# AdaLN-conditioned ternary FFN on one core: loops of four engines written out, x halves, gathers and an opening reordered

## The chip, the cores and the metric

The kernel runs on one core of one Trainium2 chip. The metric is device microseconds of an execution: 975.07 us is the median of 3 runs of the kernel before (974.96 to 975.81). Engines are named as in the profile: PE (matmul), PEld (its weight loads), DVE, ACT, POOL, SP, the last three also as issuers of DMAs.

## The reference, cut to what matters

```
w  = weights[conditions]                       # B=128 conditions pick from 200 matrices 64x64
c  = einsum('bct,bcd->bdt', x, w)              # x: 128 x 64 x 512
h  = gelu(einsum(c, ternary(W1)) + b1)         # W1: 2048 x 512
y  = einsum(h, ternary(W2)) + b2               # W2: 512 x 2048
scale = max|y| / 7 + 1e-8                      # one scale for the whole tensor
out = x + clip(round(y / scale), -7, 7) * scale
```

`ternary(W)` is alpha * sign(W) where |W| exceeds 0.05 * max|W|, and 0 elsewhere; alpha is the mean of |W| over the elements that pass. The scale needs every y before any output can be written, so the kernel has a long middle that makes y, and a tail that rounds, adds x and stores.

## The kernel before, in words

The 8192 rows (128 samples x 64) are cut in 16 blocks of 512 rows. For each block PE does a **conditioning** (line 500, in two halves of four samples, 32 matmuls of 128x64 each: psC from xs and ws), a **first product** (line 520, 128 matmuls of 128x512, 16 hidden tiles, four PSUM banks in turn) and a **second product** (lines 530, 581 and 674, 128 matmuls of 128x512). For blocks 2 to 12 the second product is made by seven half-size products in Strassen's manner (line 632, `seven`), 7 times 32 matmuls of 128x256, from sums of quarters of h that DVE and ACT build beside the first product (`hidden_seven`). Values are split in a high and a low fp16 part (`high_x`, `low_x`, `high_c`, `low_c`, and so on: ACT makes the high part, DVE the low part).

Steps are numbered by i; step i uses block i and conditions block i + 1. `seven_step(i, s)` on PE is: condition(i+1, 0), three products, one more, condition(i+1, 1), the other products. Then the first product of block i + 1 follows. PE's program is written out in full; in SP, POOL, ACT and DVE the steps i = 2 to 10 are one `Fori` loop with the step number in a register.

What each step needs from elsewhere:

- **x halves.** SP loads x of a half block (`load_half`, two DMAs of 512 KB, line 309) into `yx` (first halves) or `xd1`, which is block 14 of y (second halves of the loop). In the opening all of half blocks 0 to 4 (counted from block 2) go into `yx` one after another, each load waiting for `x_split` of the half before, which is the end of `low_x` on DVE. ACT's `sum_x` waits for the load, POOL's `all_max_x` for that, DVE's `scale_xw`, ACT's `high_x` and DVE's `low_x` follow.
- **Gathers.** POOL gathers the 64x64 matrices of four samples at a time (`gather`, lines 401 and 405: one copy of indices, four indirect DMAs) into `wg`, half 0 or half 1. In `seven_step` the order is: all_max_x(2i), gather of half 1 for block i + 2, all_max_x(2i+1), wait for x_split 2i+1, gather of half 0 for block i + 3. For the two last such steps (`LATE_X`, i = 11 and 12) POOL waits for x_split 2i and gathers half 1 first.
- **t sums.** `hidden_seven` on ACT may begin only when DVE has passed the end of the step before (line 1354 raises t_added, raw_split and m_read after `block_step(1)`).

The **opening**: ACT's queue loads the condition numbers broadcast to 128 partitions (`condb`, line 706) and b1, SP loads W1 in eight pieces, x of blocks 0 and 1 (`load_direct`), W2 and x half 0. DVE turns the condition numbers into row indices (lines 1047 to 1054), POOL gathers for blocks 0 and 1 (`gather_direct`, line 411). DVE takes max|W1| (line 1060), makes masks (line 1079) and ternary weights (line 1087); ACT takes |W1| (774), sums of relu (778), spreads the gathered matrices (721, 722) and makes the high part of c0 (716), DVE the low part (997). POOL's `all_max(xwb_part ...)` gives the bound for c0's scale. PE does condition_direct of block 0, counts the masks (`count1`, line 541), tile 0 of the first product, condition_direct of block 1, and so on.

The **tail**: the output is made in `PIECES` in block order. A piece is rounded (ACT line 915, or DVE line 1407 for pieces 0, 1 and 3), x is added (DVE line 1420), and SP stores it (line 392). `CUT` says which blocks are cut: block 0 in four pieces, blocks 1, 11 and 12 in two, the others are one piece of 1 MB. ACT's queue loads x of the last three blocks (line 913) into the places of blocks 0 to 2, each ahead of the last piece of the block two further on and after that earlier block's own addition.

Of the kernel before, what the change touches and what calls it, by code (L numbers as in the profile page):

```python
# [8 lines left out]
I32 = mybir.dt.int32  # L9
# [9 lines left out]
def build(nc, x, cond, wcond, W1, b1, W2, b2, out):  # L19
# [47 lines left out]
    with ctx:  # L67
# [6 lines left out]
        def sem(name):  # L74
            return ctx.enter_context(nc.semaphore(name))
# [22 lines left out]
        odd_i = odd[:, 2 * BB * C:].bitcast(I32)  # L98
        condb, idx, ids = odd_i[:, 0:B], odd_i[:, B:2 * B], odd_i[:, 2 * B:2 * B + BB]
        idsd = odd_i[:, 2 * B + BB:2 * B + BB + DIRECT * RT].rearrange("p (b r) -> p b r", b=DIRECT)  # L100
# [22 lines left out]
        CUT = {0: [(slice(m, m + 1), slice(n, n + 1)) for m in (0, 1) for n in (0, 1)],  # L123
               1: [(slice(m, m + 1), ALL) for m in (0, 1)],
               11: [(slice(m, m + 1), ALL) for m in (0, 1)],
               12: [(slice(m, m + 1), ALL) for m in (0, 1)]}
# [74 lines left out]

        idt = g[:, 3, 0:B].bitcast(I32)
        slots = iter(range(128))
# [29 lines left out]
        psY = ps[:, HB + 2:, :]  # L233
        psC0 = psY[:, :, :].rearrange("p i (k r) -> p (i k) r", k=KT // 2)
        psN1, psN2 = psH[:, HB - 1, :], ps[:, HB, 0:1]
        psY0 = [psY[:, 0, :], psY[:, 1, :], psH[:, 2, :], psH[:, 3, :]]
# [12 lines left out]
        w_gathered = [sem("w_gathered0"), sem("w_gathered1")]  # L249
        pool_waited = sem("pool_waited")  # L250
        consts_made, idx_made, ids_made = sem("consts_made"), sem("idx_made"), sem("ids_made")
        zero_made = sem("zero_made")
# [48 lines left out]
        def _(sp):  # L301
# [96 lines left out]
        def _(pool):  # L398
# [17 lines left out]
            gather_direct(0, range(RT))  # L416
            gather_direct(1, range(0, 2))

# [26 lines left out]
            all_max_x(1)  # L445

            def columns(b):
                return idx[:, bass.ds(b * BB, BB)]

            def block_step(i):  # L450
# [20 lines left out]
            gather(4, columns(4), [0])  # L471
            with pool.Fori(2, NS) as i:
                seven_step(i)
# [15 lines left out]
        def _(pe):  # L489
# [56 lines left out]
            def count2(c):  # L546
# [16 lines left out]
            for j in range(HT):  # L563
                if j == 0:
                    pe.wait_ge(t1_begun, 1)
                else:
                    pe.wait_ge(t1_made, j // HC + 1)
                if j == HB - 1:
                    pe.wait_ge(n_read, 1)
                first(0, j, wait_bank=j >= HB, wait_c=False)  # L570
                if j == 0:
                    pe.wait_ge(xdirect_loaded[1], 16)
                    pe.wait_ge(w_spread, 2)
                    condition_direct(1, 0, psC)
                    condition_direct(1, 1, psC0)
# [129 lines left out]
        def _(act):  # L705
            act.dma_start(condb[:, :], cond.rearrange("(a b) -> a b", a=1).to_broadcast([P, B])).then_inc(cond_loaded, 16)
            act.dma_start(b1t[:, :], b1).then_inc(b1_loaded, 16)
# [79 lines left out]
            for c in range(LOADS):  # L787
                absolute(c)
            act.dma_start(b2b[:, :], b2.rearrange("(a n) -> a n", a=1).to_broadcast([P, T])).then_inc(b2_loaded, 16)
            act.wait_ge(diagonal_cleared, 1)  # L790
# [13 lines left out]
            relu1(2)  # L804
            relu1(3)
            act.wait_ge(relu_summed, WCH)

# [57 lines left out]
            def seven_step(i, s):  # L865
                high_c(i + 1, 0)
                high_t(s, HALF_H - 1)
                sum_x(0, loads=s + 5)
                high_x(2 * i, 0)
                high_c(i + 1, 1)  # L870
                sum_x(1, xd1, xd1_loaded, s + 1)
# [23 lines left out]
            for i in range(2 + NS, NB - 2):  # L895
                second_step(i, 2 * i - (NS + 1), xd=xlate[0])
                hidden(i + 1, rb=i + 1 - NS)
# [21 lines left out]
        def _(dve):  # L919
# [126 lines left out]
            dve.wait_ge(cond_loaded, 16)  # L1046
            link(nc.vector.tensor_scalar(idt, condb[:, :], 0.0, float(S), ALU.is_lt, ALU.mult))
            link(nc.vector.tensor_tensor(idt, idt, condb[:, :], ALU.add))
# [13 lines left out]
            for c in range(LOADS):  # L1062
                last = max_w1(c)
                if c == 0:
                    dve.wait_ge(b1_loaded, 16)
                    nc.vector.tensor_reduce(xwb[:, 2:3], b1t[:, :], AX.X, ALU.max, apply_absolute_value=True)
# [46 lines left out]
            ternary1(2)  # L1113
            dve.wait_ge(relu_summed, WCH)
# [9 lines left out]
            link(nc.vector.tensor_scalar(alpha1d, alpha1, 2.0, None, ALU.mult))  # L1124
            scale_h(link, direct=True)

            def max_w2(c):
# [66 lines left out]
            def beside_second(j):  # L1194
# [4 lines left out]
                if j == 9:  # L1199
                    low_x(1, 1)  # L1200
                    scale_c(link)
# [146 lines left out]

            block_step(1, 1, *tiles_of(1), link, beside=last_sums)

# [4 lines left out]
            dve.sem_inc(m_read, 1)  # L1355

            def in_loop(i, begin, count):
                done = [0]

                def lk(ins):  # L1360
                    done[0] += 1
                    ins.then_inc(dve_step, 1)
                    dve.wait_ge(dve_step, count * i + (steps[0] - count * begin + done[0]))

                return lk, done

# [9 lines left out]
            hidden_seven(2, 0, link)  # L1376
            STEPS = 18
            with dve.Fori(2, NS) as i:
                lk, done = in_loop(i, 2, STEPS)
                seven_step(i, i - 2, *quarter_of(i), lk)  # L1380
                hidden_seven(i + 1, i - 1, lk)
                assert done[0] == STEPS, done
            steps[0] += STEPS * (NS - 2)
            owed = seven_step_late(LATE_X[0], NS - 2, *quarter_of(LATE_X[0], yx[:, :, :]), link)
# [76 lines left out]
```

## Time and profile before

| what | value |
|---|---|
| median of 3 runs | 975.07 us (974.96 to 975.81) |
| profiled execution | 974.98 us |
| its span, first to last instruction | 973.2 us |
| mean granted TensorE clock | 0.972 |
| PE busy | 892.0 us (92%) |
| DVE busy | 759.4 us (78%) |
| ACT busy | 638.2 us (66%) |
| POOL busy | 163.1 us (17%) |
| DMA bytes | 78.57 MB |

The profile is of one execution. Its busy shares are means over stages with different limits, so the stages are read one by one: in the timeline and the chain of waits each row has its start in us from the span's start, its length, its engine and line, and in brackets the idle time of the engine just before and what ended it. A matmul's end is modelled; the distance between the starts of two groups is the safer measure.

### The profile page before, as it was taken

How to read it: one execution, taken by the hardware profiler on the slowest of the kernel's cores; microseconds unless marked ns; L12 is line 12 of the kernel's file. 1: busy time of each engine (PE TensorE's matmuls, PEld its weight loads, DVE VectorE, ACT ScalarE, POOL GpSimd, SP SyncE). 2: the span in 40 equal slices, each digit the busy share in tenths (PEclk: the TensorE clock that was granted, in tenths of full speed). 3: DMA queues.
4: the chain of work that ended last, by engine and by line, in shares of the span. 5: the costliest groups of instructions: out<-in, count | busy, mean ns of one | idle time of the engine just before them, and what ended most of it. 6: DMA issues, size and time to landing. Idle time of an engine off the chain costs nothing.

```text
span 973.2 us, 16130 instructions
## 1 busy us (share of the span) xinstructions
PE 892.0 (92%) x6192; PEld 542.2 (56%) x6192; DVE 759.4 (78%) x1245; ACT 638.2 (66%) x718; POOL 163.1 (17%) x185
## 2 busy tenths in 40 slices
PE   2999999999999999999999999999999999999600
PEld 2544444766758484766758484857667444444300
DVE  7997859899797979799897979898797465433494
ACT  6787946668494958668494958666685836335191
POOL 4400231120303012121304021140410300000000
PEclk9999999999999999999999999999999999999855
DMA  9501222220304031221304040203013230204899
GB/s 338 171 3 32 50 62 47 51 49 18 81 1 97 1 74 25 50 50 27 72 1 98 1 87 12 50 11 74 22 30 64 54 87 1 87 1 156 310 388 398
DMA packets 24508, 78.57 MB, mean 81 GB/s; under 512 B 3968, under 2 KB 4096, under 8 KB 23936
## 3 DMA queue, kind: packets, MB, share of 16 engines
q1 hardware_dynamic: 19360, 70.26, 24.6%
q0 software_dynamic: 3840, 3.94, 1.6%
q10 hardware_dynamic: 1248, 3.48, 1.0%
q8 instruction: 48, 0.79, 0.3%
q14 instruction: 12, 0.10, 0.0%
HBM read 60.89 MB, written 16.78 MB: 80 GB/s over the span
## 4 chain that ended last, share of the span: by engine, by line
PE 61%; issue 18%; DVE 11%; ACT 4%; DMA 3%; POOL 1%; DVEq 0%; SPq 0%; ACTq 0%; POOLq 0%
PE ps L520 31%; PE ps L632 27%; PE ps L500 2%; ACT y L784 1%; DMA yx<-in_x 1%; DVE hs L981 1%; DVE st L1060 1%; DVE st L1129 1%; ACT xs L735 1%; DVE y L1250 1%; DMA y<-in_x 1%; DVE xs L1026 1%; DVE y L1420 1%; ACT g L752 1%; DMA odd<-in_itok_B 1%
## 5 line engine op out<-in xcount | busy, mean ns | idle before, releaser
L520 PE MATMUL ps<-yc,wts 128*128 128x512 f16 x2048 | 445.0, 379 | 1.9 <-ACT g L856 1.4
L520 PEld LDWEIGHTS ps<-yc,wts 128*128 128x128 fp8e4 x2048 | 200.2, 98 | 241.6 <-ACT g L856 1.9
L856 ACT ACTIVATE g<-ps,b1t,st 128x512 f32<-128x512 f32 x176 | 134.3, 770 | 43.6 <-PE ps L520 33.7
L405 POOL DMA_INDIRECT odd<-in_L_cond_weights,odd x112 | 133.9, 1195 | 50.4 <-issue 33.2
L632 PE MATMUL ps<-y,hs 128*128 128x256 fp8e4 x1056 | 118.9, 273 | 0.0
L1235 DVE SCALAR_TENSOR_TENSOR hs<-y,st,hs 128x1024 f16<-128x1024 f32 x88 | 112.5, 1278 | 0.0
L632 PEld LDWEIGHTS ps<-y,hs 128*128 128x128 f16 x1056 | 102.6, 98 | 11.7
L846 ACT ACTIVATE hs<-y,st 128x1024 f16<-128x1024 f32 x88 | 100.0, 1137 | 10.7 <-DVE y L1259 10.7
L422 POOL PARTITION_ALL_REDUCE st<-st x32 | 13.8, 430 | 532.5 <-DVE st L1003 404.1
L752 ACT ACTIVATE g<-ps,b1t,st 128x512 f32<-128x512 f32 x80 | 62.2, 778 | 58.4 <-PE ps L520 48.2
L981 DVE SCALAR_TENSOR_TENSOR hs<-g,st,hs 128x512 f16<-128x512 f32 x80 | 58.7, 750 | 47.7 <-ACT hs L757 46.6
L1250 DVE SCALAR_TENSOR_TENSOR y<-g,st,y 128x768 f16<-128x768 f32 x88 | 89.0, 1011 | 0.2 <-ACT y L861 0.2
L861 ACT ACTIVATE y<-g,st 128x768 f16<-128x768 f32 x88 | 82.4, 936 | 4.1 <-DVE odd L1028 1.3
L530 PE MATMUL ps<-wts,hs 128*128 128x512 fp8e4 x384 | 83.9, 379 | 0.0
L632 PE MATMUL ps<-wts,y 128*128 128x256 fp8e4 x704 | 78.8, 273 | 0.4 <-DVE y L1250 0.3
L632 PEld LDWEIGHTS ps<-wts,y 128*128 128x128 f16 x704 | 68.1, 98 | 8.4 <-DVE y L1250 0.4
L728 ACT ACTIVATE xs<-y,st 128x2048 f16<-128x2048 f32 x15 | 30.0, 2001 | 57.6 <-DVE st L1011 57.6
L1245 DVE TENSOR_TENSOR y<-g 128x512 f32<-128x512 f32 x88 | 60.3, 685 | 2.4 <-ACT g L856 1.1
L746 ACT ACTIVATE yc<-ps,st 128x1024 f16<-128x1024 f32 x28 | 30.9, 1103 | 47.4 <-PE ps L500 47.4
L530 PEld LDWEIGHTS ps<-wts,hs 128*128 128x128 f16 x384 | 37.1, 98 | 43.9
L757 ACT ACTIVATE hs<-g,st 128x512 f16<-128x512 f32 x80 | 56.7, 715 | 0.0
L1270 DVE SCALAR_TENSOR_TENSOR y<-ps,st,b2b 128x512 f32 (+1 forms) x40 | 29.9, 748 | 25.8 <-PE ps L632 25.7
(167 smaller groups left out, 981.1 us busy)
## 6 DMA issues: line engine op xcount, KB each, us to landing
y<-in_x SPq DMA_DIRECT2D x30, 512.0 KB, 7.1
yx<-in_x SPq DMA_DIRECT2D x26, 512.0 KB
y<-in_L_ffn_W SPq DMA_DIRECT2D x8, 512.0 KB, 7.5
y<-in_L_ffn_W SPq DMA_DIRECT2D x4, 1024.0 KB, 20.5
hs<-in_x SPq DMA_DIRECT2D x8, 512.0 KB, 5.0
out<-hs SPq DMA_DIRECT2D x8, 512.0 KB, 12.4
y<-in_x ACTq DMA_DIRECT2D x3, 1024.0 KB, 10.2
out<-y SPq DMA_DIRECT2D x3, 1024.0 KB, 13.9
```

What stands on the lines that cost most here:

```text
L405: nc.gpsimd.indirect_dma_start(out=wg[:, j, :], out_offset=None, in_=w_rows[:, :], in_offset=bass.IndirectOffsetOnAxis(ap=ids[:, j:j + 1], ...
L520: last = nc.tensor.matmul(psH[:, j % HB, :], weights, csp[:, a, k, :], start=(k == 0 and a == 0), stop=(k == KT - 1 and a == 1))
L530: last = nc.tensor.matmul(psY[:, r % 2, :], hsp[:, a, j, r * P:(r + 1) * P], T2T[:, j, :], start=(j == 0 and a == 0), stop=(j == HT - 1 an ...
L632: last = nc.tensor.matmul(psM[bank][:, t * HALF_T:(t + 1) * HALF_T], rows[:, a, p, at:at + P], weights[:, p, :], start=(first_of_bank and ...
L752: nc.scalar.activation(g[:, j % HB, :], psH[:, j % HB, :], ACT.Gelu, bias=b1t[:, j:j + 1], scale=ascale).then_inc(g_made, 1)
L846: nc.scalar.activation(told[:, 0, p, :], tsum[:, p % 2, :], ACT.Copy, scale=s_h).then_inc(thi_made, 1)
L856: nc.scalar.activation(g[:, q % HB, :], psH[:, q % HB, :], ACT.Gelu, bias=b1t[:, q:q + 1], scale=ascale).then_inc(g_made, 1)
L861: nc.scalar.activation(raw[:, :, 0, p, :], gp[:, p % 2, HALF_T:].rearrange("p (q w) -> p q w", q=3), ACT.Copy, scale=s_h).then_inc(rhi_mad ...
L981: nc.vector.scalar_tensor_tensor(out=hsp[:, 1, j, :], in0=g[:, j % HB, :], scalar=s_h, in1=hsp[:, 0, j, :], op0=ALU.mult, op1=ALU.subtract ...
L1235: nc.vector.scalar_tensor_tensor(out=told[:, 1, p, :], in0=tsum[:, p % 2, :], scalar=s_h, in1=told[:, 0, p, :], op0=ALU.mult, op1=ALU.subt ...
L1245: nc.vector.tensor_tensor(at[:, 0:2 * HALF_T].rearrange("p (s t) -> p s t", s=2), gp[:, p % 2:p % 2 + 1, 0:HALF_T].to_broadcast([P, 2, HAL ...
L1250: nc.vector.scalar_tensor_tensor(out=raw[:, :, 1, p, :], in0=gp[:, p % 2, HALF_T:].rearrange("p (q w) -> p q w", q=3), scalar=s_h, in1=raw ...
```

## The change

- The `Fori` loops of SP, POOL, ACT and DVE over steps 2 to 10 become Python loops, so that their instructions are written out.
- x: half 1 goes to `xd1` as soon as ACT's four relu sums are made (they used that place); then half 2 to `yx` after x_split 1, half 3 to `xd1` after x_split 2, half 4 to `yx` after x_split 3.
- POOL: the gather of half 0 for block 3 comes after x_split 1, ahead of all_max_x(1); in `seven_step` the gather of half 1 for block i + 2 comes first, after a wait for x_split 2i.
- Step 1 of ACT and DVE is written out in an order of its own; DVE's `max_y(1, 0)`, `last_sums(0)` and `max_w(3)` change places.
- Opening: condition numbers are loaded once, into one partition; three DVE operations on that row; a matmul with one row of ones spreads it over 128 partitions in PSUM (`psIds`); DVE's last index operation reads it there. POOL gathers three tiles of block 1 before the maxima, and the fourth behind `all_max(xwb_part ...)`. ACT's load of b2 moves behind relu1(3). `mask_w1(3)` moves behind c0's low part, `count1(3)` behind tile 0 of the first product, `ternary1(2)` behind `scale_h`, the maximum of b1 behind the second W1 piece.
- Tail: blocks 2 and 3 are cut in two pieces each.

```diff
@@ CUT
                1: [(slice(m, m + 1), ALL) for m in (0, 1)],
+               2: [(slice(m, m + 1), ALL) for m in (0, 1)],
+               3: [(slice(m, m + 1), ALL) for m in (0, 1)],
@@ SP
             load_half(2 * DIRECT)
-            for n in range(1, 5):
+            sp.wait_ge(relu_summed, WCH)
+            load_half(1 + 2 * DIRECT, xd1, xd1_loaded)
+            for n in range(1, 4):
                 sp.wait_ge(x_split, n)
-                load_half(n + 2 * DIRECT)
-            with sp.Fori(2, NS - 1) as i:
+                if n % 2:
+                    load_half(n + 1 + 2 * DIRECT)
+                else:
+                    load_half(n + 1 + 2 * DIRECT, xd1, xd1_loaded)
+            for i in range(2, NS - 1):
@@ POOL
             gather_direct(0, range(RT))
-            gather_direct(1, range(0, 2))
+            gather_direct(1, range(0, 3))
...
             all_max(max1_part, 1, m1r, m1, max1_all)
-            gather_direct(1, range(2, RT))
             pool.wait_ge(x0_summed, 1)
             all_max(xwb_part, 1, xwbr, xwb, xwb_all)
+            gather_direct(1, range(3, RT))
...
             all_max_x(0)
+            pool.wait_ge(x_split, 1)
+            gather(2, columns(3), [0])
             all_max_x(1)
...
             def seven_step(i):
+                pool.wait_ge(x_split, 2 * i)
+                gather(2 * i + 1, columns(i + 2), [1])
                 all_max_x(2 * i)
-                gather(2 * i + 1, columns(i + 2), [1])
                 all_max_x(2 * i + 1)
                 pool.wait_ge(x_split, 2 * i + 1)
                 gather(2 * i + 2, columns(i + 3), [0])
-            pool.wait_ge(x_split, 2)
-            gather(2, columns(3), [0])
             all_max_x(2)
...
-            with pool.Fori(2, NS) as i:
+            for i in range(2, NS):
                 seven_step(i)
@@ PE
+            pe.wait_ge(id_row_made, 1)
+            nc.tensor.matmul(psIds, ones_f[0:1, :], id_row, start=True, stop=True).then_inc(ids_spread, 1)
...
-            for c in range(WCH):
+            for c in range(WCH - 1):
                 count1(c)
+            pe.wait_ge(idx_made, 1)
...
                 if j == 0:
+                    count1(WCH - 1)
                     pe.wait_ge(xdirect_loaded[1], 16)
@@ ACT
-            act.dma_start(condb[:, :], cond.rearrange("(a b) -> a b", a=1).to_broadcast([P, B])).then_inc(cond_loaded, 16)
+            act.dma_start(cond_row, cond.rearrange("(a b) -> a b", a=1)).then_inc(cond_loaded, 16)
...
                 if j == 4:
-                    sum_x(1, loads=2)
+                    sum_x(1, xd1, xd1_loaded, 1)
                 if j == 8:
-                    high_x(1, 1)
+                    high_x(1, 1, xd1)
...
-            second_step(1, 3)
+            high_c(2, 0)
+            sum_x(0, loads=2)
+            high_x(2, 0)
+            high_c(2, 1)
+            sum_x(1, xd1, xd1_loaded, 2)
+            high_x(3, 1, xd1)
             hidden_seven(2, 0)
-            with act.Fori(2, NS) as i:
+            for i in range(2, NS):
@@ DVE
-            link(nc.vector.tensor_scalar(idt, idt, 0.0, float(S - 1), ALU.max, ALU.min))
-            link(nc.vector.tensor_scalar(idx[:, :], idt, float(C), pc64, ALU.mult, ALU.add))
+            nc.vector.tensor_scalar(id_row, idt, 0.0, float(S - 1), ALU.max, ALU.min).then_inc(id_row_made, 1)
+            dve.wait_ge(ids_spread, 1)
+            link(nc.vector.tensor_scalar(idx[:, :], psIds, float(C), pc64, ALU.mult, ALU.add))
...
-            mask_w1(3)
             ternary1(0, slice(0, 1), t1_begun)
             dve.wait_ge(cscale_ready, 1)
             low_c0(0, psC)
             low_c0(1, psC0)
+            mask_w1(3)
...
-            block_step(1, 1, *tiles_of(1), link, beside=last_sums)
+            scale_h(link)
+            low_c(2, 0)
+            max_w(2, 0, 3)
+            scale_xw(2, 0, link)
+            store_y(1, 0, tile_y(0))
+            low_x(2, 0)
+            low_c(2, 1)
+            max_y(1, 0, tile_y(0), slot(0))
+            store_y(1, 1, tile_y(1))
+            max_y(1, 1, tile_y(1), slot(1))
+            last_sums(0)
+            max_w(3, 1, 3)
+            scale_xw(3, 1, link)
+            store_y(1, 2, tile_y(2))
+            max_y(1, 2, tile_y(2), slot(2))
+            low_x(3, 1, xd1)
+            scale_c(link)
+            last_sums(1)
+            store_y(1, 3, tile_y(3))
+            max_y(1, 3, tile_y(3), slot(3))
...
-            with dve.Fori(2, NS) as i:
-                lk, done = in_loop(i, 2, STEPS)
-                seven_step(i, i - 2, *quarter_of(i), lk)
-                hidden_seven(i + 1, i - 1, lk)
+            for i in range(2, NS):
+                seven_step(i, i - 2, *quarter_of(i), link)
+                hidden_seven(i + 1, i - 1, link)
```

## Rows read from the trace of the kernel before

**Rows 1.** The page, busy time of PE (and its weight loads).

```profile
PE 892.0 (92%) x6192; PEld 542.2 (56%) x6192; DVE 759.4 (78%) x1245; ACT 638.2 (66%) x718; POOL 163.1 (17%) x185
```

**Rows 2.** Waits of PE: line, releaser, us in total, times, longest.

```profile
PE ps L520 <- ACT g L856: 1.4, 1, 1.4
PE ps L581 <- ACT g L752: 0.8, 2, 0.6
```

**Rows 3.** The chain of waits: start us, us, what; from step 2 to step 12.

```profile
191.81 0.81 PE ps L500 x27
...
194.05 10.48 PE ps L632 x96
204.53 27.63 PE ps L520 x128
232.16 0.93 PE ps L500 x32
...
639.38 27.63 PE ps L520 x128
...
693.33 27.63 PE ps L520 x128
...
747.27 27.64 PE ps L520 x128
```

**Rows 4.** Timeline of PE, from step 1 to step 2.

```profile
146.85 7.07 PE L520 MATMUL ps<-yc,wts 128*128 128x512 f16 x32
...
204.37 27.79 PE L520 MATMUL ps<-yc,wts 128*128 128x512 f16 x128
```

**Rows 5.** The chain of waits inside step 1.

```profile
133.12 6.96 DMA yx<-in_x
140.10 2.01 ACT xs L735 x2
...
143.84 2.30 DVE y L1192
...
154.47 1.46 ACT g L856 x2
```

**Rows 6.** DMA queues while step 3 conditions, 246.4 to 248.7 us.

```profile
q0 software_dynamic: 104, 0.10, 17.5%
```

**Rows 7.** DMA queues while step 11 conditions, 681.2 to 682.9 us.

```profile
q1 hardware_dynamic: 86, 0.31, 88.5%
```

**Rows 8.** Timeline of POOL ahead of step 11: first and last gather of half 1.

```profile
644.01 0.97 POOL L405 DMA_INDIRECT odd<-in_L_cond_weights,odd  x1 [0.81 <-POOL odd L401]
...
648.27 1.09 POOL L405 DMA_INDIRECT odd<-in_L_cond_weights,odd  x1 [0.30 <-issue]
```

**Rows 9.** Stretches of the tail: engines busy, PEclk, DMA share, GB/s.

```profile
926.00:930.00 4.00, 0.00 (x0) 0.00 (x0) 3.85 (x2) 3.17 (x3) 0.00 (x0) 0.50 0.95 273
930.00:972.00 42.00, 0.00 (x0) 0.00 (x0) 28.34 (x15) 23.35 (x14) 0.00 (x0) 0.50 1.02 419
```

**Rows 10.** Timeline of DVE in the tail: block 2's addition.

```profile
926.12 2.35 DVE L1420 SCALAR_TENSOR_TENSOR xs<-y,st,xs 128x2048 f32<-128x2048 int16 x1 [0.26 <-ACT y L915]
```

**Rows 11.** Stretches of the opening, columns as in Rows 9.

```profile
2.50:5.50 3.00, 0.00 (x0) 0.00 (x0) 0.87 (x5) 0.65 (x2) 0.00 (x0) 1.00 0.67 188
5.50:8.50 3.00, 0.00 (x0) 0.00 (x0) 2.20 (x7) 2.09 (x2) 0.58 (x1) 1.00 1.03 401
```

**Rows 12.** Timeline of the opening.

```profile
18.70 5.34 PE L508 MATMUL ps<-odd,hs 128*128 128x128 f32 x32 [18.70 <-DMA hs<-in_x]
...
19.88 2.41 POOL L411 DMA_INDIRECT odd<-in_L_cond_weights,odd  x1 [0.30 <-issue]
...
27.73 0.41 ACT L721 ACTIVATE odd<-odd 64x256 f32<-64x256 f32 x1
```

**Rows 13.** Waits of DVE between 195 and 640 us.

```profile
DVE y L1270 <- PE ps L632: 41.8, 25, 2.9
```

**Rows 14.** The page, instruction packets of the queue that isn't PE's.

```profile
q14 instruction: 12, 0.10, 0.0%
```

More of the change, by code:

```diff
@@ L98, in build @@
         odd_i = odd[:, 2 * BB * C:].bitcast(I32)
-        condb, idx, ids = odd_i[:, 0:B], odd_i[:, B:2 * B], odd_i[:, 2 * B:2 * B + BB]
+        cond_row, idx, ids = odd_i[0:1, 0:B], odd_i[:, B:2 * B], odd_i[:, 2 * B:2 * B + BB]
         idsd = odd_i[:, 2 * B + BB:2 * B + BB + DIRECT * RT].rearrange("p (b r) -> p b r", b=DIRECT)
@@ L200, in build @@
         xtail += [place(y[:, b, :, :].rearrange("p r t -> p (r t)")) for b in range(NB - XS)]
-        idt = g[:, 3, 0:B].bitcast(I32)
+        idt, id_row = g[0:1, 3, 0:B].bitcast(I32), g[0:1, 3, B:2 * B]
         slots = iter(range(128))
@@ L234, in build @@
         psC0 = psY[:, :, :].rearrange("p i (k r) -> p (i k) r", k=KT // 2)
+        psIds = psH[:, 0, 0:B]
         psN1, psN2 = psH[:, HB - 1, :], ps[:, HB, 0:1]
@@ L250, in build @@
         pool_waited = sem("pool_waited")
+        id_row_made, ids_spread = sem("id_row_made"), sem("ids_spread")
         consts_made, idx_made, ids_made = sem("consts_made"), sem("idx_made"), sem("ids_made")
@@ L444, in _ @@
             all_max_x(0)
-            all_max_x(1)
             def columns(b):
                 return idx[:, bass.ds(b * BB, BB)]
+            pool.wait_ge(x_split, 1)
+            gather(2, columns(3), [0])
+            all_max_x(1)
             def block_step(i):
@@ L788, in _ @@
                 absolute(c)
-            act.dma_start(b2b[:, :], b2.rearrange("(a n) -> a n", a=1).to_broadcast([P, T])).then_inc(b2_loaded, 16)
             act.wait_ge(diagonal_cleared, 1)
@@ L805, in _ @@
             relu1(3)
+            act.dma_start(b2b[:, :], b2.rearrange("(a n) -> a n", a=1).to_broadcast([P, T])).then_inc(b2_loaded, 16)
             act.wait_ge(relu_summed, WCH)
@@ L867, in seven_step @@
                 high_t(s, HALF_H - 1)
-                sum_x(0, loads=s + 5)
+                sum_x(0, loads=s + 3)
                 high_x(2 * i, 0)
                 high_c(i + 1, 1)
-                sum_x(1, xd1, xd1_loaded, s + 1)
+                sum_x(1, xd1, xd1_loaded, s + 3)
                 high_x(2 * i + 1, 1, xd1)
-            second_step(1, 3)
+            high_c(2, 0)
[4 more added lines that the diff above has]
+            high_x(3, 1, xd1)
             hidden_seven(2, 0)
-            with act.Fori(2, NS) as i:
+            for i in range(2, NS):
                 seven_step(i, i - 2)
@@ L895, in _ @@
             for i in range(2 + NS, NB - 2):
-                second_step(i, 2 * i - (NS + 1), xd=xlate[0])
+                second_step(i, 2 * i - (NS + 3), xd=xlate[0])
                 hidden(i + 1, rb=i + 1 - NS)
@@ L1046, in _ @@
             dve.wait_ge(cond_loaded, 16)
-            link(nc.vector.tensor_scalar(idt, condb[:, :], 0.0, float(S), ALU.is_lt, ALU.mult))
-            link(nc.vector.tensor_tensor(idt, idt, condb[:, :], ALU.add))
-            link(nc.vector.tensor_scalar(idt, idt, 0.0, float(S - 1), ALU.max, ALU.min))
-            link(nc.vector.tensor_scalar(idx[:, :], idt, float(C), pc64, ALU.mult, ALU.add))
+            link(nc.vector.tensor_scalar(idt, cond_row, 0.0, float(S), ALU.is_lt, ALU.mult))
+            link(nc.vector.tensor_tensor(idt, idt, cond_row, ALU.add))
+            nc.vector.tensor_scalar(id_row, idt, 0.0, float(S - 1), ALU.max, ALU.min).then_inc(id_row_made, 1)
+            dve.wait_ge(ids_spread, 1)
+            link(nc.vector.tensor_scalar(idx[:, :], psIds, float(C), pc64, ALU.mult, ALU.add))
             by_tile = idx[:, 0:DIRECT * BB].rearrange("p (b r s) -> p s b r", b=DIRECT, s=2)
@@ L1063, in _ @@
                 last = max_w1(c)
-                if c == 0:
+                if c == 1:
                     dve.wait_ge(b1_loaded, 16)
@@ L1112, in _ @@
             ternary1(1)
-            ternary1(2)
             dve.wait_ge(relu_summed, WCH)
@@ L1125, in _ @@
             scale_h(link, direct=True)
+            ternary1(2)
             def max_w2(c):
@@ L1199, in beside_second @@
                 if j == 9:
-                    low_x(1, 1)
+                    low_x(1, 1, xd1)
                     scale_c(link)
@@ L1347, in last_sums @@
                     nc.vector.tensor_tensor(wsum[:, 3], A12, wsum[:, 1], ALU.subtract, saturate=False).then_inc(w2_summed, 1)
-            block_step(1, 1, *tiles_of(1), link, beside=last_sums)
+            tile_y, slot = tiles_of(1)
+            scale_h(link)
[18 more added lines that the diff above has]
+            max_y(1, 3, tile_y(3), slot(3))
             dve.wait_ge(h_split, 2 * HT)
@@ L1355, in _ @@
             dve.sem_inc(m_read, 1)
[L1357 to L1365, printed above, removed]
             def quarter_of(b, place=None):
@@ L1376, in _ @@
             hidden_seven(2, 0, link)
-            STEPS = 18
-            with dve.Fori(2, NS) as i:
-                lk, done = in_loop(i, 2, STEPS)
-                seven_step(i, i - 2, *quarter_of(i), lk)
-                hidden_seven(i + 1, i - 1, lk)
-                assert done[0] == STEPS, done
-            steps[0] += STEPS * (NS - 2)
+            for i in range(2, NS):
+                seven_step(i, i - 2, *quarter_of(i), link)
+                hidden_seven(i + 1, i - 1, link)
             owed = seven_step_late(LATE_X[0], NS - 2, *quarter_of(LATE_X[0], yx[:, :, :]), link)
```

## The prediction

> **What bounds the kernel now.** I read the busy times first, then PE's waits, then the chain of waits, and last the timelines around each place where PE stood. PE is busy 92% of the span [rows 1]. It starts at 18.70 us, when x of block 0 has landed [rows 12], and from then to its last product it hardly stands: its waits on other engines that matter are one of 1.4 us and two of 0.8 us together [rows 2]. So an edit counts only if it lets PE start sooner, fills a hole in PE's row, or shortens the tail behind PE; whatever other engines gain counts nothing by itself.
>
> The holes that PE's list of waits does not name are read from the distance between first products. From 639.38 to 693.33 and on to 747.27 a step takes 53.95 and 53.94 us: the clean step. From 204.53 to 639.38 there are eight steps, 434.85 us, where eight clean ones take 431.56: 3.29 us of holes [rows 3]. The step before is longer still: 146.85 to 204.37, 57.52 us, 3.57 too many [rows 4]. Inside it the second conditioning takes 194.05 - 191.81 = 2.24 us where an undisturbed one takes 0.93, so 1.31 of the 3.57 lie there; the other 2.26 lie ahead of it [rows 3].
>
> **The gathers.** In steps 2 to 10 POOL's gather of half 1 runs beside the second conditioning: 104 of its packets pass in 2.3 us around that of step 3 [rows 6]. In step 11, where POOL gathers half 1 well ahead (644.01 to 649.4) [rows 8], the x load keeps the DMA engines 88.5% busy beside the conditioning and no gather packet is there [rows 7], and that step is clean. So I put 3.29 + 1.31 = 4.60 us on the gathers, nine conditionings, about 0.5 each. The new order in `seven_step` is the one that steps 11 and 12 have: the gather of half 1 starts as soon as DVE has finished with that half, tens of us ahead of the conditioning, as in step 11 (649.4 against 681.2 or later). The instructions are the same. In front of POOL's next maximum there are now four more gathers, about 5 us, but that maximum waits for an ACT sum that comes much later. Term: 4.60 us; below, 0 if the cause is another.
>
> Trainium skill, SBUF — State Buffer, section "SBUF: two separate sides": engines and DMAs reach the memory by ports of their own, and a transfer cannot slow an engine. By that, gathered data landing would not hold PE, and this term would be 0. The rows of steps 3 and 11 speak for a tie to the gathers by whatever path, not necessarily the memory; I go with the rows and keep the rule as a rival.
>
> **Second x halves.** Step 1's chain is serial: a load of x half 3 that starts at 133.12 and lands at 140.08, ACT's sum of 2.01, scale, high and low part, two DVE sums of 2.30 each, then ACT's first gelu at 154.47 [rows 5]. PE has made four banks by then: 146.85 plus a quarter of 27.8 is 153.8, and it stands 1.4 us [rows 2, 4]; the rest of the 2.26 are small waits in the following products, because DVE and ACT are still behind. After the change half 3 is asked for at x_split 2, one half sooner, into a place of its own. What is late next: POOL's gather of half 1 for block 3, still issued behind this step's conditioning, now beside the load of half 4. If it lands as late as the x half does today (140.08), the sum of 2.01 and one DVE sum of 2.30 no longer stand behind it; with about 1 us back for the maximum of w, the gelu starts near 151.2. It needs to be done by 153.8. So all of 2.26 goes; the other bound, 0, needs the gather 3 us later than that.
>
> **Tail.** Behind PE the end is set by DMAs: 419 GB/s from 930 on, but 273 from 926 to 930, where only loads run while block 2's single piece is being added, 2.35 us [rows 9, 10]. Halved, its first 512 KB can leave half of 2.35, 1.2 us, earlier, and 1.2 x (419 - 273) / 419 = 0.4 us of transfer time comes back. At best the whole stretch runs at 419, 4 x 146 / 419 = 1.4. The loads of the last x blocks are asked for up to 0.5 us later, because ACT now does half pieces ahead of them: at worst -0.2. I take 0.4, the value of the one piece that moves.
>
> **Opening.** (a) The condition numbers, 128 rows of them, go beside W1's first pieces: from 2.5 to 5.5 us the DMAs move 188 GB/s, and 401 afterwards [rows 11]. At the full rate the loads would be 3 x 213 / 401 = 1.6 us ahead, and PE's start waits for such a load [rows 12]. But part of the slow stretch may be the start itself: 0 to 1.6, I take half, 0.8. The hop over PE and PSUM (an operation that no row shows, bounded by 0 and the 2.4 us that gathers have in hand) only delays gathers that nothing waits for: they start sooner than today. (b) The eighth gather moves behind `all_max(xwb)`: today it is issued at 19.88 and read at 27.73 without idle time before it [rows 12], so it takes at most 7.85 us to land. All_max, which runs behind it today at 22.3, goes first; the gather is then issued between 20.3 and 22.7. I take 21.2, since ACT's sum over x is then what all_max waits for; it lands by 29.1, up to 1.4 late for ACT's spread, and so for the relu sums, alpha and DVE's ternary weights, which PE's second product waits for. Between 0 and -1.4; I take -0.5, nearer to 0 since the landing came some time before the read. b2's later load is needed much later, and masks, counts and ternary parts are the same instructions in another order. Sum: +0.3, from -1.4 to +1.6.
>
> Trainium skill, DMA: Bandwidth & Descriptors, section "Queues, rings and completion order": each engine takes turns between queues packet by packet. By that the eighth gather would not stand behind the W2 load, (b) would cost nothing and the sum would be 0.5 us better; no row here shows the landing itself.
>
> **Written-out loops.** PE had no loop. The other four lose their branches, which costs or gains nothing as long as they keep ahead of PE; DVE alone stood 41.8 us waiting for PE's products between 195 and 640 [rows 13]. Term 0.
>
> **Sum.** 4.60 + 2.26 + 0.4 + 0.3 = 7.56. The profiled execution took 974.98 us, 1.8 more than its span, and gives 967.4; the median of the runs is 0.09 higher, so 967.5.
>
> **Rivals.**
> 1. The holes in the conditionings have another cause and stay: 967.5 + 4.6 = 972.1. For it: a coincidence in time is all that the rows show. Against: steps 11 and 12 are clean under the very order that is now used everywhere. The page on SBUF would have it so. Chance 0.09.
> 2. Step 1 stays late: the gather for half 1 of block 3 lands behind the load of half 4, PE stands again for its 2.3: 969.8. Against: 3 us in hand. Chance 0.08.
> 3. The opening loses: W1 starts no sooner and the eighth gather holds ACT by its full 1.4: 967.5 + 0.3 + 1.4 = 969.2. Chance 0.10.
> 4. Slower. Written out, the instruction streams of ACT and DVE in steps 2 to 10 must be fetched anew in every step, where the loops came back to code already there; today 12 such packets carry 0.10 MB in the whole run [rows 14]. If each step's fetch held DVE or ACT beyond what they have in hand, PE would stand in all nine steps. DVE's waits give 41.8 / 9 = 4.6 us in hand a step [rows 13]; a hold of 5.8 would cost 1.2 a step, 967.5 + 9 x 1.2 = 978.3. It turns the sign from 0.85 a step beyond that. Against: the written-out opening and tail show no DVE or ACT waits of such a size without a named releaser. Chance 0.04.
>
> **Chances.** The forecast has 0.69, with an own range of 966.1 to 969.0. What a measurement of this kernel can tell from no change is about 0.2%, 1.95 us, so faster means under 973.1. Rival 1 is faster mostly, with its neighbours in "same": faster 0.92, same 0.04, slower 0.04. For 8 in 10 I reach over rivals 2 and 3, to 970.2, and down to 966.0, which needs the opening at its better bound.
>
> **What would show it.** Right: every second conditioning of steps 2 to 10 at 0.93 us and all first products 53.9 us apart; no PE wait on ACT's gelu near 153; store rate in the first 10 us of the tail higher by a third in one 4 us stretch; PE's first matmul a little ahead of 18.70. Wrong: holes of 0.3 to 0.7 us left in the conditionings without gather packets beside them (rival 1); a gelu after 153.8 (rival 2); ACT idle before its second spread (rival 3); DVE or ACT rows with idle time that no other engine released, once a step (rival 4). The prediction fails if the time is above 970.2.

## The result, and the profile after

After: 967.99 us median of four runs (967.76 to 968.14), before 975.02 beside it (974.93 to 975.81): ratio 0.9926, 95% interval 0.9909 to 0.9943. The forecast was 967.5, with 966.0 to 970.2. The profiled execution took 968.06, its span 966.1; all comparisons of traces below are between spans.

The page first: PE has the same work but for two matmul records of the hop (L569, the matmul that spreads the condition numbers), and 1.0 us less of modelled busy time [rows 1]; the rest of the 7.1 us that the span lost was idle.

```profile
PE 891.0 (92%) x6194; PEld 542.5 (56%) x6194; DVE 762.2 (79%) x1247; ACT 639.9 (66%) x720; POOL 164.9 (17%) x185
```

PE's waits. The two holes named in [rows 2] were L520 waiting for ACT's gelu (1.4) and L581 (0.8); L533 and L599 are these lines now. The 1.4 is gone; what is left lies ahead of 62 us (L569 stands for the condition numbers and L521 for x, both at the start).

```profile
PE ps L521 <- DMA hs<-in_x: 12.2, 1, 12.2
PE ps L569 <- DVE g L1072: 4.2, 1, 4.2
PE ps L599 <- ACT g L770: 1.1, 2, 0.9
PE ps L599 <- issue: 0.6, 1, 0.6
PE ps L533 <- issue: 0.2, 1, 0.2
```

The chain of waits (start, us), first products L533 and second conditionings L513, against [rows 3].

```profile
146.46 27.63 PE ps L533 x128
...
188.99 0.93 PE ps L513 x32
200.40 27.63 PE ps L533 x128
...
242.94 0.93 PE ps L513 x32
254.35 27.63 PE ps L533 x128
...
685.92 27.63 PE ps L533 x128
...
739.87 27.64 PE ps L533 x128
```

Every step from 146 to 740 us is now 53.94 or 53.95 long, the length that steps 11 and 12 had before, and all conditionings take 0.93. Two marks on PE divide the 7.1 us. The first is the point from which block 0's second product runs on: that product begins at 58.45 (before 59.27), stands for ACT twice, and goes on steadily from its 13th matmul. The second is the start of the last product of all. Before, then after:

```profile
63.04 18.30 PE L581 MATMUL ps<-wts,hs 128*128 128x512 fp8e4 x84 [0.24 <-ACT g L752]
...
888.98 27.79 PE L674 MATMUL ps<-wts,hs 128*128 128x512 fp8e4 x128
```

```profile
62.49 18.30 PE L599 MATMUL ps<-wts,hs 128*128 128x512 fp8e4 x84 [0.24 <-ACT g L770]
...
881.57 27.79 PE L692 MATMUL ps<-wts,hs 128*128 128x512 fp8e4 x128
```

Opening 0.55, middle 6.86, tail -0.3. The last is no more than noise: from the start of the last product to the end it is 84.52 us here, 84.01 in the second trace of the same kernel (`e10_after_again`), and 84.18 before.

Step 1, against [rows 5]: ACT's gelu starts at 149.66 instead of 154.47. DVE waits 2.22 us there for POOL's gather, as the prediction said would be late next, and is still over 3 us ahead of PE's need.

```profile
149.66 1.45 ACT L874 ACTIVATE g<-ps,b1t,st 128x512 f32<-128x512 f32 x2 [6.86 <-DVEq L1398]
```

```profile
138.57 0.42 DVE L1026 TENSOR_REDUCE st<-odd 128x1 f32<-128x256 f32 x1 [2.22 <-DMA odd<-in_L_cond_weights,odd]
```

The opening: stretches (last column GB/s), against [rows 11]; then PE, ACT and DVE, against [rows 12].

```profile
2.50:5.50 3.00, 0.79 (x2) 0.49 (x2) 1.81 (x10) 1.71 (x3) 0.00 (x0) 1.00 1.02 382
5.50:8.50 3.00, 0.00 (x0) 0.00 (x0) 2.96 (x6) 2.21 (x4) 2.04 (x2) 1.00 1.02 411
```

```profile
17.22 5.65 PE L521 MATMUL ps<-odd,hs 128*128 128x128 f32 x32 [12.19 <-DMA hs<-in_x]
...
31.84 2.54 PE L533 MATMUL ps<-yc,wts 128*128 128x512 f16 x11
```

```profile
26.95 0.42 ACT L739 ACTIVATE odd<-odd 64x256 f32<-64x256 f32 x1 [0.89 <-DMA odd<-in_L_cond_weights,odd]
```

```profile
23.10 2.48 DVE L1020 SCALAR_TENSOR_TENSOR yc<-ps,st,yc 128x1024 f16<-128x1024 f32 x2 [0.54 <-ACT yc L734]
...
31.93 0.16 DVE L1138 TENSOR_REDUCE st<-st 128x1 f32<-128x4 f32 x1 [0.52 <-ACT y L796]
```

The loads run at 382 GB/s from the start, PE begins 1.48 earlier, and still only 0.55 reaches the mark at 62.49 us. From 32 to 59 us the chain of waits runs mostly over DVE, and ahead of that DVE stands twice: 0.54 for ACT's high part, 0.52 for ACT's last relu sum, which in turn stands behind 0.89 of waiting for the eighth gather.

The tail's slow stretch after, and in the experiment in which blocks 2 and 3 stay whole (`e4_cut_back`). Each window begins 37.41 us after the start of that trace's last product; the same window of before, 926.39 to 930.39, has 285 GB/s ([rows 9] begin 0.39 us earlier).

```profile
918.98:922.98 4.00, 0.00 (x0) 0.00 (x0) 4.00 (x4) 2.85 (x2) 0.00 (x0) 0.50 0.94 299
```

```profile
918.40:922.40 4.00, 0.00 (x0) 0.00 (x0) 3.96 (x2) 3.47 (x2) 0.00 (x0) 0.50 0.94 295
```

The halves move 299 GB/s, the whole blocks 295: the halves don't lift the slow stretch.

### The profile page after: what moved, and what is told of

The parts are those of the page before. It is cut to its first block, busy times and chain, and to the rows that moved or that the text cites. A ratio compares the mean times of both kernels' runs of the same rounds, so it can differ in the third digit from the quotient of the medians.

```text
span 966.1 us, 15274 instructions
## 1 busy us (share of the span) xinstructions
PE 891.0 (92%) x6194; PEld 542.5 (56%) x6194; DVE 762.2 (79%) x1247; ACT 639.9 (66%) x720; POOL 164.9 (17%) x185
## 4 chain that ended last, share of the span: by engine, by line
PE 73%; issue 16%; DVE 5%; DMA 2%; ACT 1%; SPq 0%; POOL 0%; DVEq 0%; POOLq 0%; ACTq 0%
PE ps L533 37%; PE ps L650 28%; PE ps L543 3%; PE ps L599 3%; PE ps L513 2%; DMA hs<-in_x 1%; DVE st L1153 1%; DVE y L1450 1%; DVE hs L1004 1%; DMA y<-in_x 1%; DVE wts L1111 0%; SPq L321 0%; DVE hs L1450 0%; POOL st L432 0%; ACT g L770 0%
## 5 line engine op out<-in xcount | busy, mean ns | idle before, releaser
L533 PE MATMUL ps<-yc,wts 128*128 128x512 f16 x2048 | 444.8, 379 | 0.2 <-issue 0.2
L533 PEld LDWEIGHTS ps<-yc,wts 128*128 128x128 fp8e4 x2048 | 200.2, 98 | 239.6 <-issue 0.7
L746 ACT ACTIVATE xs<-y,st 128x2048 f16<-128x2048 f32 x17 | 34.0, 2001 | 66.4 <-DVE st L1034 66.4
L1294 DVE SCALAR_TENSOR_TENSOR y<-ps,st,b2b 128x512 f32<-128x512 f32 x40 | 29.9, 748 | 31.9 <-PE ps L650 31.9
```

The lines of the kernel that those rows point to most:

```text
L533: last = nc.tensor.matmul(psH[:, j % HB, :], weights, csp[:, a, k, :], start=(k == 0 and a == 0), stop=(k == KT - 1 and a == 1))
```

## The experiments

The kernels ran in three groups, each on a chip of its own; before took 975.41, 973.15 and 973.11 us there. Two sets of runs of before in the third group have medians 0.35 apart, so less than about 0.4 us says nothing. "Holes" are what the nine second conditionings take beyond 0.93 each, from the starts of their matmuls: 4.61 us in the first trace of before.

**First group.** `e1_gather_back`: after, with the old order in POOL's `seven_step`.

```diff
-                pool.wait_ge(x_split, 2 * i)
-                gather(2 * i + 1, columns(i + 2), [1])
                 all_max_x(2 * i)
+                gather(2 * i + 1, columns(i + 2), [1])
```

> The changed kernel with POOL's old order in seven_step alone (gather of half 1 behind the first maximum). If gather packets beside the second conditioning hold PE: the nine conditionings of steps 2 to 10 lose about 0.5 us each again and the time is 968.0 + 4.6 = 972.6 us. If the holes came from the loops of the other engines or from the x loads that land there: no holes, 968.0 us.

Measured 969.36 (968.87 to 970.27). The holes come back, but 2.1 us and not 4.6: three of 0.50 to 0.56, six of 0 to 0.23. The chain shows one:

```profile
242.43 0.67 PE ps L512 x23
243.50 0.42 PE ps L512 x9
```

`e2_only_gather`: the same edit alone, forward, in before.

> The kernel before with the new order of POOL's gathers in seven_step alone, its loops kept. If the gathers hold PE: 975.0 - 4.6 = 970.4 us with nine clean conditionings of 0.93 us. If the loops or the x loads do: 975.0 us, holes as before.

Measured 970.57 (969.91 to 971.01), 4.84 less than before, for a term of 4.60. All nine are clean, while step 1 keeps its wait of 1.5 us on ACT's gelu. In step 3:

```profile
245.85 1.10 PE L501 MATMUL ps<-odd,xs 128*128 128x64 f16 x32
246.78 2.46 PE L633 MATMUL ps<-y,hs 128*128 128x256 fp8e4 x21
```

So the order is enough by itself; but in after, undoing it costs only 1.7 (against 967.66 of `e4_cut_back`, which stands for after in this group). Something else in the change does part of the same work; `e6_loops_only` looks for it.

`e3_x_back`: after, with the x loads and step 1 of before (SP's `load_half(n + 2 * DIRECT)` behind x_split n, `block_step(1)` and `second_step(1, 3)`).

> The changed kernel with the x halves loaded one after another into one place and step 1 of ACT and DVE in the old order; gathers, loops, opening and tail stay. If PE's hole behind step 1 was the late x half: 968.0 + 2.3 = 970.3 us, first gelu of step 2 about 5 us later and a PE wait of about 1.4 us on it. If the gather's new place is what matters: 968.0 us.

Measured 969.50 (969.12 to 970.84). ACT's gelu of step 2 is at 153.30 again, and PE's wait on it is back; with small holes behind it step 1 is 2.29 us longer than a clean one in the trace, 1.8 by the medians (against `e4_cut_back`).

```profile
PE ps L528 <- ACT g L869: 1.4, 1, 1.4
```

`e4_cut_back`: after, without the two new lines of `CUT`.

> The changed kernel with blocks 2 and 3 in one piece each again. If the halves bring transfer time back, as the prediction had it: 968.0 + 0.4 = 968.4 us. If the first store waits for the x load ahead of it anyway, as the trace of after suggests (issued 1.4 us earlier against the scale, packets at the same place): 967.7 to 968.0 us.

Measured 967.66 (967.26 to 968.03): the halves bring nothing.

**Second group.** `e5_gather_first`: after, with the gather held back so that its packets fall around the first conditioning, where no x load runs.

```diff
                 pool.wait_ge(x_split, 2 * i)
+                pool.wait_ge(h_summed, HT * i + 13)
                 gather(2 * i + 1, columns(i + 2), [1])
```

> After, with one more wait in POOL's step: the gather of half 1 is held until ACT and DVE have handed over tile 13 of the next hidden block, so that its packets pass beside the FIRST conditioning of the following step, where no x load is under way. Theory 1 (gather packets beside a conditioning hold PE): nine first conditionings grow from 0.93 to between 1.2 and 1.6 us, 9 x 0.45 = 4.0, so 972.0 us; the second conditionings stay at 0.93. Theory 2 (the load of x, or only its coincidence with the gather, holds PE): all conditionings stay at 0.93 and the time at 968.0.

Measured 967.25 (967.03 to 967.45), all conditionings 0.93. In step 3 the packets of its third indirect DMA of four begin to move 1.07 us after the conditioning's start, those of the fourth and last at 2.6, too late to count, so `e9_gather_at_first` repeats it better placed.

`e6_loops_only`: before, with the four `Fori` loops written out and nothing else.

> Before, with only the four loops written out, everything else as it was. The prediction gave this part 0: 975.4, with second conditionings of 1.3 to 1.6 us as before. Theory from the run that put the old gather order back into after: written out, POOL issues the gather a little earlier against the conditioning, the holes shrink to about half (their excess 4.6 to 2.1), so 975.4 - 2.5 = 972.9. Rival 4 of the prediction (instructions fetched anew hold ACT or DVE): above 975.4, to 978.

Measured 972.63 (972.10 to 973.01), ratio 0.9994 (0.9985 to 1.0003): at most 1.5 us, perhaps nothing. Its holes are 1.79 us; before's on a chip of the same speed are 2.88 (`e12_before_again`). The last indirect DMA starts 0.70 us ahead of the conditioning of step 3, as in `e1_gather_back`, and 0.58 in both traces of before.

`e7_cond_wide`: after, with the condition numbers broadcast to 128 partitions.

```diff
-            act.dma_start(cond_row, cond.rearrange("(a b) -> a b", a=1))
+            act.dma_start(condb[:, :], cond.rearrange("(a b) -> a b", a=1).to_broadcast([P, B]))
...
-            dve.wait_ge(ids_spread, 1)
-            link(nc.vector.tensor_scalar(idx[:, :], psIds, float(C), pc64, ALU.mult, ALU.add))
+            link(nc.vector.tensor_scalar(idx[:, :], idt, float(C), pc64, ALU.mult, ALU.add))
```

> After, with the condition numbers loaded to 128 partitions again and the four index operations on DVE without the product in PSUM. The prediction's opening (a): PE's first matmul back at about 18.7 (after: 17.2) and W1's loads slow until 5.5 us again. Theory 1 (most of PE's earlier start is given back, as DVE's chain sets the second product): the end moves by 0.3 to 0.6, so 968.4. Theory 2 (PE's start is the end, as the prediction reckoned): 968.0 + 1.5 = 969.5.

Measured 969.42 (968.58 to 970.40), 2.2 above `e5_gather_first` beside it. The early stretch is back at 186 GB/s and PE's start at 19.09 (there: 16.99), and the difference of 2.1 reaches the end whole, so my first theory here is wrong. That PE's start by itself counts is not shown: the loads of W1 are late too, and DVE's first mask begins 1.92 later (18.58, there 16.66).

```profile
2.50:5.50 3.00, 0.00 (x0) 0.00 (x0) 0.85 (x5) 0.64 (x2) 0.00 (x0) 1.00 0.60 186
```

```profile
19.09 6.23 PE L521 MATMUL ps<-odd,hs 128*128 128x128 f32 x32 [19.09 <-DMA hs<-in_x]
```

`e8_both`: after, with all eight opening gathers in one row and `mask_w1(3)` at its old place, ahead of `ternary1(0, slice(0, 1))`.

> After, with the eighth gather ahead of the maxima again (all eight in one row) and the fourth mask ahead of the ternary parts, as before. Theory 1 (in after's opening DVE stands 0.54 and 0.52 us for ACT, which stands 0.89 for the eighth gather, and 1.28 of mask stands behind c0's low part): PE's second product of block 0 starts 0.5 to 1.1 earlier, 967.1. Theory 2 (something else sets that start, such as the loads of W1 or the maxima): 968.0. Theory 3 (eight gathers in one row delay POOL's maximum of W1): slower by up to 1.0, 969.0.

Measured 968.07 (967.64 to 968.70), 0.8 above `e5_gather_first`. The mask was made early, but its count still stood behind tile 0 on PE, and DVE waited for it (below). Theory 3 has a small part: POOL's maximum of W1 now stands behind eight gathers, and DVE's first mask begins at 16.86 instead of 16.66.

```profile
29.14 0.69 DVE L1134 TENSOR_REDUCE st<-ps 128x1 f32<-128x512 f32 x1 [1.16 <-PE ps L553]
```

**Third group.** `e9_gather_at_first`: as `e5_gather_first`, with `HT * i + 12`, so that the gather is released one tile sooner.

> After, with POOL's gather of half 1 held until tile 12 of the next first product: 1.7 us sooner than in the run that held it to tile 13, so that the fourth and last of its indirect DMAs is issued about 1 us ahead of the FIRST conditioning and lands inside it, as it did in the second conditionings of the kernel before, but with no x load having just ended. Theory 1 (a gather's last indirect DMA that lands beside narrow matmuls holds PE by itself): eight or nine first conditionings of 1.2 to 1.5 us instead of 0.93, together 2.5 to 5 us, so 969.7 to 972. Theory 2 (the hold needs the end of the x load too, whose packets delay the gather's): all conditionings 0.93, and the time of after, 967.2.

Measured 967.57 (967.46 to 968.39); all conditionings 0.93. Here it stands beside `e12_before_again`. First the kernel before around the second conditioning of step 3: the timeline of PE and POOL, and the gather's queue from 247.8 to 248.2 us.

```profile
246.69 0.98 PE L500 MATMUL ps<-odd,xs 128*128 128x64 f16 x28
247.97 0.29 PE L500 MATMUL ps<-odd,xs 128*128 128x64 f16 x4 [0.30 <-issue]
...
246.11 0.95 POOL L405 DMA_INDIRECT odd<-in_L_cond_weights,odd  x1 [0.31 <-issue]
```

```profile
q0 software_dynamic: 26, 0.02, 16.8%
```

The same of `e9_gather_at_first` around a first conditioning, the queue from 282.8 to 283.2.

```profile
281.72 1.10 PE L514 MATMUL ps<-odd,xs 128*128 128x64 f16 x32
...
280.80 1.28 POOL L415 DMA_INDIRECT odd<-in_L_cond_weights,odd  x1 [0.30 <-issue]
```

```profile
q0 software_dynamic: 28, 0.02, 20.4%
```

In both the packets of the last indirect DMA begin to move some 1.1 us after the conditioning's start (in five of the nine steps of `e9_gather_at_first`; in the other four those of the third do). In the first PE stands half a microsecond, in the second not at all. What differs lies just ahead: in the microsecond before the conditioning, 245.7 to 246.7, the x load of the kernel before ends and a heap of gather packets that had waited behind it passes; in `e9_gather_at_first`, 280.7 to 281.7, only the gather's own third DMA. The queues of that microsecond, in that order of kernels:

```profile
q0 software_dynamic: 86, 0.10, 44.9%
q1 hardware_dynamic: 26, 0.04, 22.0%
```

```profile
q0 software_dynamic: 32, 0.03, 9.2%
```

`e10_after_again`: after, unchanged.

> After, unchanged, on the chip and beside the runs of this call: 967.2 to 968.0, for comparing the others. Its second product of block 1 (first conditioning for block 2) begins near 116.3 by the traces of three relatives, near 116.8 if its own first profile was typical.

Measured 967.66 (967.18 to 968.04), ratio 0.9944 (0.9931 to 0.9958): here the change is worth 5.45 us, not 7.0.

`e11_order_back`: after, with mask, count and ternary part of the opening at their places of before, and blocks 2 and 3 whole.

```diff
-            for c in range(WCH - 1):
+            for c in range(WCH):
                 count1(c)
...
-                    count1(WCH - 1)
...
+            mask_w1(3)
             ternary1(0, slice(0, 1), t1_begun)
...
-            mask_w1(3)
             ternary1(0, slice(1, HC))
...
             ternary1(1)
+            ternary1(2)
...
             scale_h(link, direct=True)
-            ternary1(2)
```

> After, with the fourth mask, the fourth count and the third ternary part back at their places of before, and blocks 2 and 3 in one piece; the narrow condition load and the gathers stay as in after. The prediction gave the order of masks, counts and ternary parts 0. Theory 1 (that order costs: from PE's start to the first conditioning for block 2 it is 98.7 us in kernels with the opening of before, 99.2 in those with the new one): 0.5 faster by the order, 0.2 by the pieces, so 0.7 below after. Theory 2 (the order is worth nothing either way): 0 to 0.3 below after. Theory 3 (it gains, as the run with both the eighth gather and the fourth mask put back suggests): 0.3 to 0.6 above after.

Measured 966.64 (965.94 to 967.30), 1.02 below `e10_after_again` beside it, ratio to before 0.9933 (0.9919 to 0.9946): the fastest kernel of the study, ahead of both. DVE's first low part of h, in this kernel and in `e10_after_again`:

```profile
38.32 0.75 DVE L1001 SCALAR_TENSOR_TENSOR hs<-g,st,hs 128x512 f16<-128x512 f32 x1
```

```profile
39.07 0.75 DVE L1004 SCALAR_TENSOR_TENSOR hs<-g,st,hs 128x512 f16<-128x512 f32 x1
```

DVE is 0.75 ahead although PE began 0.56 later there (17.77 against 17.21): the mask fills the 0.54 in which DVE stood for ACT, the third ternary part the 0.39 in which it stood for the relu sums, and the count is made before it is asked for.

`e12_before_again`: before, unchanged.

> Before, unchanged, for a second profile: the run with only the loops written out came on a chip where before took 973.2 and not 975.4. Theory 1 (the size of the holes in the second conditionings depends on a few tenths of a us in when the gather lands, so it differs from chip to chip): where before takes about 973, its conditionings have 2 to 3 us of holes and not 4.6; where it takes 975.4, they have 4 to 5. Theory 2 (the chips differ elsewhere): 4.6 us of holes in either case.

Measured 973.46 (972.50 to 974.46). Its holes are 2.88 us, not 4.61: 1.7 less, and its median is 1.6 less than before's in the first comparison. The last indirect DMA lands at about the same place in both traces (its packets begin 1.07 to 1.08 us after the conditioning's start in step 3); the hole is 0.64 there and 0.48 here.

## Why the prediction was right, point by point

**Gathers, 4.60.** Size and cure were right where before takes 975: 4.61 of holes in the trace, 4.84 by the one edit. As a constant of the kernel it was wrong: on the third chip the same holes are 2.88, and the change is worth 1.6 less. The mechanism that I had in mind, that gather packets beside a conditioning hold PE, failed too. In step 3 of before PE begins its 24th matmul at 247.57 and its 25th at 248.24, where the others are 0.03 apart. The packets that had waited behind the x load passed beside the first of these 24 and held none; from 247.35 to 247.90 no packet of any queue moves. Nor did PE wait for its instructions: neither instruction queue (q8, q14) brings a packet between 239.4 and 250.1.

```profile
246.90 0.86 PE L500 MATMUL ps<-odd,xs 128*128 128x64 f16 x24
248.24 0.39 PE L500 MATMUL ps<-odd,xs 128*128 128x64 f16 x8 [0.48 <-issue]
```

In step 4 of `e6_loops_only` gather packets move inside the conditioning (the queue from 301.01 to 301.94), just behind an x load, and it is clean:

```profile
301.01 1.10 PE L500 MATMUL ps<-odd,xs 128*128 128x64 f16 x32
301.94 0.82 PE L632 MATMUL ps<-y,hs 128*128 128x256 fp8e4 x6
```

```profile
q0 software_dynamic: 36, 0.03, 11.0%
```

Gather without x load: nine clean conditionings (`e9_gather_at_first`). x load without gather: clean in after, and in steps 11 and 12 of before with the queue 88.5% busy [rows 7]. Only a gather caught behind an ending x load, with its last DMA landing in the conditioning or just behind it, left PE standing, and not every one; the order in POOL removes that meeting. What the size goes with is how far ahead of the conditioning POOL begins the last indirect DMA. In `e6_loops_only`: 1.37 us ahead no hole (five steps), 0.70 ahead 0.33 to 0.39 (three), 0.24 ahead 0.69. In `e12_before_again`: 1.25 ahead 0 to 0.19 (five), 0.57 ahead 0.45 to 0.54 (three), 0.16 behind 1.09. In all 24 holes of 0.07 us or more in these two traces, the first of before and `e1_gather_back`, PE goes on 1.81 to 2.01 us after that DMA was begun, while its packets move: the end of a hole hangs on that DMA. By the rule on ports of the Trainium skill (SBUF — State Buffer, section "SBUF: two separate sides") neither stream should hold PE; each alone agrees with it, and the 0.5 us of the two together it does not explain. `e9_gather_at_first` moved the gather to the first conditioning, which follows wide products of 512 columns and not of 256; so the place is not told apart from the missing load. There POOL also begins the DMA 0.92 ahead and not 0.57; between the rows of `e12_before_again` that would be a hole of about 0.25 (an estimate), and that is what its clean steps speak against. By what path PE is held stays open, and so does why the same landing costs 0.64 on one chip and 0.48 on another.

**Second x halves, 2.26.** Right: 2.29 in the trace of `e3_x_back`, 1.8 by its time. The gather was what came late next, the gelu at 149.66 and not 151.2.

**Tail, +0.4.** Worth nothing: whole blocks were no slower (`e4_cut_back`), and from the last product's start to the end the eight traces with halves have a mean of 84.20 us, the six with whole blocks 84.21. The step that failed: that an earlier store fills the slow stretch. Block 2's first store is issued 38.1 us after the last product's start instead of 39.5 (919.68 after, 928.50 before), yet that stretch moves 299 GB/s, with whole blocks 295. What holds it there no run shows.

**Opening, +0.3.** The sum was nearly right (0.55 in the first traces, 0.77 in the third group) by two errors. (a) 0.8 for the narrow load was about half of it: nearly all of 188 against 401 GB/s in [rows 11] was the broadcast. PE begins 1.48 earlier, and put back into after the wide load costs 2.1 to 2.2 (`e7_cond_wide`), even more than the upper bound of 1.6. One reading was wrong here: the hop was said to delay only gathers that nothing waits for, with 2.4 us in hand, which no row shows. In before ACT stood 1.15 us for them, and its second spread ended at 18.53, 0.17 ahead of PE's first matmul:

```profile
17.70 0.42 ACT L721 ACTIVATE odd<-odd 64x256 f32<-64x256 f32 x1 [1.15 <-DMA odd<-in_L_cond_weights,odd]
```

It did no harm, since the gathers begin at 6.08 instead of 7.92. (b) -0.5 was put on the eighth gather. It did make ACT stand 0.89 (in `e5_gather_first`, with the same opening, not at all); but the larger loss came from the masks, counts and ternary parts, which the prediction priced at nothing as "the same instructions in another order". They cost 0.75 by the first mark in the traces (62.40 in `e10_after_again`, 61.65 in `e11_order_back`) and 1.02 by the times, which have the whole blocks in them: the order left DVE idle on the path that sets the second product. The page DMA: Bandwidth & Descriptors of the Trainium skill (section "Queues, rings and completion order") would have the gather not wait behind the W2 load; it was issued at 20.96 and its reader released at 26.95, 6.0 us, so the trace gives that hope no support.

**Written-out loops, 0.** Nearly right: 0.5, with 0 inside its interval, and no sign of rival 4, though instruction packets of that queue rose from 12 to 22 against [rows 14]:

```profile
q14 instruction: 22, 0.18, 0.1%
```

What the prediction missed is that loops and gather order work on the same holes: written out, POOL begins the gather's last DMA 0.12 us earlier against the conditioning, and the holes are 1.79 (`e6_loops_only`) and not 2.88 (`e12_before_again`). When only the order was put back (`e1_gather_back`), 2.5 of the 4.61 us stayed away. 1.4 of them lie in steps 3 to 10, which have those 0.12; 1.1 lie in step 2, where the DMA is begun 1.16 us ahead of the conditioning instead of 0.16 behind it. The loops alone bring that to 0.24 ahead; which other part of the change does the rest no run tells apart.

On the third chip the account closes like this: holes 2.88, step 1 2.14, opening 0.77, tail 0.1, together 5.9; the spans are 971.4 and 965.5. That the time came within 0.5 us of the forecast is in part luck: the tail's 0.4 didn't come, the opening gave up to half a microsecond more than its term, and the change was worth 7.0 us only where before takes 975.

## What to carry to other kernels

A hole that ends without a named releaser is best sized by the distance between repeats of the same product, and cured by moving apart the transfers that meet there; its size is not a constant: a tenth of a microsecond in the meeting, or another chip, took more than a third off it here. Reordering equal instructions is free only where the engine has idle time ahead of it: where one engine runs without a gap up to the next product, list what it will stand for in the new order. Edits that remove the same hole must not be added up, nor be judged by undoing one of them.

## What was not expected of the hardware

- With a load of 512 B to each of 128 partitions among them, all loads together moved 186 to 188 GB/s in 3 us of the opening; with one row of it 382 to 388.
- The same kernel took 975.4 on one chip and 973.1 on two others; of the difference of 2.3 us the holes account for 1.7, and what does the rest is not known. After and the kernels nearest to it, without these holes, differ less between chips: 967.25 to 967.99.
- An x load that kept the DMA engines 88.5% busy, and gathers landing around a conditioning, each left PE's narrow matmuls at 0.93 us. With gathers behind an ending load PE stood up to 1.31 us, and wherever it stood 0.07 us or more it went on 1.81 to 2.01 us after POOL had begun the gather's last indirect DMA; in five steps of `e6_loops_only`, with that DMA begun 1.37 us ahead, it did not stand at all.
